# The decay of a Mamba2 mixer: exponents bounded below by zero on GpSimd, one exponential a step on ScalarE

## What is computed

```python
A = -jnp.arange(1, H + 1)                          # 128 heads
dt = jnp.clip(softplus(dt + dt_bias), 0.001, 100)
cs = jnp.cumsum(dA, axis=-1)                       # in chunks of 128 tokens, dA = dt * A
seg = cs[..., :, None] - cs[..., None, :]
Lmat = jnp.where(tri, jnp.exp(seg), 0.0)           # tri: l >= s
scores = jnp.einsum('bclhn,bcshn->bchls', Cc, Bc) * Lmat
Ydiag = jnp.einsum('bchls,bcshp->bclhp', scores, xdt)
# ... the states carried from one chunk to the next, Y = Ydiag + Yoff + x * D
yg = y * silu(gate)
out = (yg * rsqrt(mean(yg ** 2 over a group) + EPS)) * norm_w @ out_proj_w.T
```

## Time and profile before

| | |
|---|---|
| median of three runs | 1798.07 us (1796.7 to 1801.74) |
| span of the profiled execution | 1797.3 us |
| mean granted TensorE clock | 0.981 of full speed |
| instructions | 27181 |
| DMA, mean | 73 GB/s, 131.86 MB |
| length of one group | 206 to 207 us |

### The profile page before, as it was taken

How to read it: one execution, slowest core, us unless ns; L and a number is a source line. 1 busy time by engine, 2 the same in 40 slices (tenths; PEclk the granted TensorE clock), 3 DMA queues, 4 the chain that set the end, 5 groups by cost and what they waited for, 6 DMA issues and landing times. The chain is left out here.

```text
span 1797.3 us, 27181 instructions
## 1 busy us (share of the span) xinstructions
PE 1615.7 (90%) x8296; PEld 1228.1 (68%) x8296; DVE 1479.8 (82%) x1833; ACT 1045.5 (58%) x2144; POOL 1123.3 (62%) x664
## 2 busy tenths in 40 slices
PE   7888989989898899989898898989899898989889
PEld 5666767767676666757676676757676676767666
DVE  6789598986979688895979778895989879895975
ACT  4556574665646565665747665564646666475632
POOL 2039584695828775595928777484936868286831
PEclk9989999999999999999999999999999999999999
DMA  2032221221223122231213222131212312122101
GB/s 107 6 111 93 73 81 56 83 83 54 83 66 100 66 71 77 72 100 53 83 44 105 83 71 77 49 105 60 91 46 83 106 43 90 51 94 82 54 14 70
DMA packets 73672, 131.86 MB, mean 73 GB/s; under 512 B 10944, under 2 KB 10944, under 8 KB 73280
## 3 DMA queue, kind: packets, MB, share of 16 engines
q1 hardware_dynamic: 73536, 130.09, 22.4%
HBM read 127.44 MB, written 2.62 MB: 72 GB/s over the span
## 5 line engine op out<-in xcount | busy, mean ns | idle before, releaser
L161 PE MATMUL bank<-h_hi,mx_w_hi 128*128 128x512 f32 x1152 | 482.2, 419 | 15.5 <-POOL mx_w_lo L834 12.4
L163 PE MATMUL bank<-h_hi,mx_w_lo 128*128 128x512 f32 x1152 | 457.5, 397 | 0.0
L162 PE MATMUL bank<-h_lo,mx_w_hi 128*128 128x512 f32 x1152 | 456.8, 397 | 0.0
L1010 POOL TENSOR_TENSOR mx_y<-mx_y,mx_sg 128x512 f32<-128x512 f32 x128 | 213.4, 1667 | 308.1 <-DVE mx_y L1258 308.1
L887 DVE SCALAR_TENSOR_TENSOR mx_acc<-bank,mx_cw,mx_acc 128x510 f32<-128x510 f32 (+2 forms) x480 | 354.5, 739 | 38.8 <-ACT mx_acc L872 33.9
L1002 POOL TENSOR_TENSOR mx_mix<-mx_csb,mx_mask 128x512 f32<-128x512 f32 x128 | 346.4, 2706 | 3.1 <-DMA mx_csb<-cs_rows 3.1
L1230 DVE TENSOR_TENSOR mx_mix<-mx_mix,mx_cbt 128x1536 f32<-128x1536 f32 x128 | 346.4, 2706 | 0.8
L834 POOL TENSOR_TENSOR mx_w_lo<-mx_w_raw,mx_w_hi 128x512 fp32r<-128x512 f32 x144 | 190.3, 1322 | 209.8 <-ACT mx_w_hi L829 209.8
L161 PEld LDWEIGHTS bank<-h_hi,mx_w_hi 128*128 128x128 f32 x1152 | 220.9, 192 | 77.6 <-issue 35.0
L163 PEld LDWEIGHTS bank<-h_hi,mx_w_lo 128*128 128x128 f32 x1152 | 220.1, 191 | 50.6
L162 PEld LDWEIGHTS bank<-h_lo,mx_w_hi 128*128 128x128 f32 x1152 | 221.1, 192 | 39.7
(11 more groups left out here) (164 smaller groups left out, 2363.8 us busy)
## 6 DMA issues: line engine op xcount, KB each, us to landing
mx_csb<-cs_rows SPq DMA_DIRECT2D x128, 512.0 KB, 3.9
mx_w_raw<-in_w_in SPq DMA_DIRECT2D x144, 256.0 KB, 3.7
mx_wo_raw<-in_w_out SPq DMA_DIRECT2D x64, 256.0 KB, 3.2
res<-in_x SPq DMA_DIRECT2D x8, 256.0 KB, 3.6
f_base_raw<-in_base_wt SPq DMA_DIRECT2D x2, 1024.0 KB, 5.9
out<-res SPq DMA_DIRECT2D x8, 256.0 KB, 2.0
f_a_raw<-in_lora_a SPq DMA_DIRECT2D x2, 256.0 KB, 3.0
f_lb_raw<-in_lora_b SPq DMA_DIRECT2D x2, 256.0 KB, 6.8
```

The source lines that it names most:

```text
L161: nc.tensor.matmul(out, w_hi, x_hi, start=first, stop=False)
L162: nc.tensor.matmul(out, w_hi, x_lo, start=False, stop=False)
L163: return nc.tensor.matmul(out, w_lo, x_hi, start=False, stop=last)
L1010: nc.gpsimd.tensor_tensor(y[:, i, :], y[:, i, :], sg[:, i, :], ALU.mult).then_inc(s["yg"], 1)
```

## The change

GpSimd no longer adds a mask. For each step it writes `max(csb - gncs, 0)` into `mix`, with eight `tensor_scalar` instructions (per head and sequence one of 256 and one of 128 elements; `gncs` is a scalar per partition), and counts `clamped`. ScalarE takes one exponential over the 1536 elements with scale -1 and no bias, in the place of `decay_from_second`; `decay_from_first` goes, and so does `mask_first` on VectorE. Where the target is before the source the exponent is now 0 and the decay 1, and the zero comes from `cbt`: `keep_bc` multiplies by a tensor `causal` of ones and zeros instead of copying. `mix` is stored head first, so that `make_mix` reads one row of 768 for each head. On GpSimd the clamps of the next step stand ahead of `gate_y`. SP's `load_cs` waits for `clamped` instead of `decay`. GpSimd's loop over the groups is written out in full; at a group's end the clamps for the next group wait for its `const`.

```diff
@@ SP
             def load_cs(g, st):
-                step_slot_freed(sp, s["decay"], g, st)
+                step_slot_freed(sp, s["clamped"], g, st)
@@ GpSimd
-            def mask_second(g, st):
-
-                i = st % 2
+            def clamp_exponents(g, st):
+
+                i, j, hf = st % 2, st // 2, st % 2
+                if st == 0:
+                    pool.wait_ge(s["const"], 1 + 5 * g + 3)
                 pool.wait_ge(cs_in[i], 16 * (STEPS // 2 * g + st // 2 + 1))
                 step_slot_freed(pool, s["y"], g, st)
-                rows = csb[:, i, :, :].rearrange("p h (b l) -> p b h l", b=HB)[:, :, :, CH:SEQ]
-                nc.gpsimd.tensor_tensor(mix[:, i, :, :, SEQ:PAIR], rows,
-                                        mask[:, :].unsqueeze(1).unsqueeze(1).to_broadcast([P, HB, 2, CH]),
-                                        ALU.add).then_inc(s["masked1"], 1)
+                for hd in range(2):
+                    for b in range(HB):
+                        tile, head = 2 * (HB * hf + b), 2 * j + hd
+                        nc.gpsimd.tensor_scalar(mix[:, i, hd, b, 0:SEQ], csb[:, i, hd, b * SEQ:(b + 1) * SEQ],
+                                                gncs[:, tile, head:head + 1], 0.0, ALU.subtract, ALU.max)
+                        last = nc.gpsimd.tensor_scalar(mix[:, i, hd, b, SEQ:PAIR],
+                                                       csb[:, i, hd, b * SEQ + CH:(b + 1) * SEQ],
+                                                       gncs[:, tile + 1, head:head + 1], 0.0,
+                                                       ALU.subtract, ALU.max)
+                last.then_inc(s["clamped"], 1)
...
                 for st in range(STEPS + 1):
+                    if st + 1 < STEPS:
+                        clamp_exponents(g, st + 1)
+                    elif st + 1 == STEPS and more:
+                        clamp_exponents(g + 1, 0)
                     if st >= 1:
                         gate_y(g, st - 1)
-                    if st + 1 < STEPS:
-                        mask_second(g, st + 1)
-                    elif st + 1 == STEPS and more:
-                        mask_second(g + 1, 0)
...
-            loop_groups(pool, group)
+            for g in range(NG):
+                group(g, g + 1 < NG)
@@ ScalarE (decay_from_first and decay_from_second are taken out)
+            def decay(g, st):
+
+                i = st % 2
+                act.wait_ge(s["clamped"], 1 + STEPS * g + st + 1)
+                a = mix[:, i, :, :, :].rearrange("p h b l -> p (h b l)")
+                nc.scalar.activation(a, a, ACT.Exp, scale=-1.0).then_inc(s["decay"], 1)
@@ VectorE (mask_first and its calls are taken out)
                 for b in range(HB):
-                    last = nc.vector.tensor_copy(cbt[:, hf, b, :], banks[b][:, 0:PAIR])
+                    last = nc.vector.tensor_tensor(cbt[:, hf, b, :], banks[b][:, 0:PAIR], causal[:, :], ALU.mult)
...
-                a = mix[:, i, :, :, :]
-                nc.vector.tensor_tensor(a, a, cbt[:, hf, :, :].unsqueeze(2).to_broadcast([P, HB, 2, PAIR]),
-                                        ALU.mult).then_inc(s["mix"], 1)
+                a = mix[:, i, :, :, :].rearrange("p h b l -> p h (b l)")
+                both = cbt[:, hf, :, :].rearrange("p b l -> p (b l)").unsqueeze(1).to_broadcast([P, 2, HB * PAIR])
+                nc.vector.tensor_tensor(a, a, both, ALU.mult).then_inc(s["mix"], 1)
```

## The result

| | before | after |
|---|---|---|
| median | 1798.4 us (1796.7 to 1801.7) | 2391.9 us (2391.5 to 2392.5) |
| ratio | | 1.3296, 95% interval 1.3277 to 1.3315 |
| span of the profiled execution | 1797.3 us | 2390.0 us |
| mean granted TensorE clock | 0.981 | 0.874 |

The account below looks back on a forecast made before the run. VectorE, nearly tied with GpSimd, was taken to bound the steps, and GpSimd after the change. 13X - 27.9 us a group at X = 2.8 is +8.5, over 8 groups +68 us: 1865 us, range 1755 to 2000.

Parts of the forecast that it names:

- What bounds the kernel before, and where the bound goes: In the steps, VectorE sets the pace with GpSimd 0.4 to 0.8 us behind; the bound moves to GpSimd.
- what would show it: Signs of being right, such as clamps starting every 0.3 and 0.4 us and steps of 9.9 and 10.4 us.
- X: Total time of the eight tensor_scalar on GpSimd in a step: 2.8 us, likely 1.75 to 4.1.
- The formula: A group changes by 13X - 27.9 us: +8.5 us at X = 2.8, +68 us for 8 groups.
- First half: From skip_y's possible start on step 0 to the first output projection: 7X + 49.3 us against 65.6.
- Second half: From skip_y's possible start on step 9 to the channel sums: 6X + 43.6 against 57.7, plus 2.5 us for the clock.
- The rest of the group stays as is: Outside the two halves, output projections on TensorE with GpSimd idle up to 11.3 us at a time: unchanged.
- y(9): The moment when skip_y can start on the step numbered in the brackets; for step 9 at 433.57 before.
- The memset's pace (1): Rival: the clamps on GpSimd run as fast as a memset, X = 1.56, giving 1717 us; chance 0.15.
- the even case (4): Rival: X on GpSimd lies within 0.05 of 2.15, so the time stays the same; chance 0.05.
- Rival 2: VectorE's hold does not stop one-input GpSimd instructions; TensorE sets the pace, 19.8 us a group saved, 1639 us; chance 0.05.
- Rival 3: The clamps on GpSimd run at the two-input pace, X = 5.3, 2125 us; chance 0.10 for X above 4.1.

Follow-up runs that it names:

- experiment 1: The changed kernel with gate_y put back ahead of the clamps on GpSimd, nothing else: 2311.9 us, ratio to before 1.2842.
- experiment 5: gate_y put first in two kernels: two-input subtractions on GpSimd with Relu on ScalarE (1956.3 to 2006.3 us), and one-operation constant clamps (2149.9 to 2136.3 us).
- experiment 3: The changed kernel with the bound formed by eight Relu on ScalarE, no clamps or mask on GpSimd: 1687.2 us, ratio to before 0.9369.

## Why the prediction was wrong, step by step

*What bounds the kernel before, and where the bound goes*: right. GpSimd without idle time in the steps, VectorE idle before tap 1 for `evacuate`, TensorE waiting more before the transposes (283.5 us against 108.1 in the earlier trace rows) and `make_mix` at 1.75 us, no longer stretched, were all on the list of what would show it.

*X*: the step that failed. It took the affine select as the nearest row because that also reads one tensor and writes one, and allowed 0.05 us each for the scalar and the second operation. The scalar was right within 0.04 us. The second operation costs per element (0.9 ns, thus 0.11 and 0.22 us), and the base was half the true one: 0.25 against 0.49 us at 128. Of the 4.4 us by which X was short, 2.8 are the base (5.20 against 2.44) and 1.6 the scalar and the second operation (2.04, where 0.4 had been allowed). Nor was the two-input pace a ceiling; the text assumed it without a row. 13 x (7.24 - 2.8) x 8 = **462 us of the 527 us** by which the forecast fell short.

*The formula*: a group becomes 206.3 + 13 x 7.24 - 27.9 = 272.5 us; the measured ones are 279.8 (from the channel sums at 363.23 to those at 642.98). For 8 groups the line gives 2328 us. With the measured X it is 2.7% short. Its pieces, in group 2 (the second of eight):

- First half: 7X + 49.3 = 100.0; measured 95.1, from `skip_y` at 406.29 to the projection at 501.39. Second half: 6X + 43.6 + 2.5 = 89.5; measured 87.8. The sums were high, for the larger part because `silu_conv` does not hold a clamp (below), 0.45 us a step. The 0.5 us for that hold was also read high from its own row: 1.66 less 1.27 is 0.39 us.
- "The rest of the group stays as is": failed. From the first projection to y(9) it was 39.3 us and is 53.8. The rows of TensorE's timeline with idle time, at its start and in it:

```profile
501.39 0.79 PE L160 MATMUL bank<-mx_wo_hi,yg_hi 128*128 128x512 f32 x1 [4.93 <-DVE mx_wo_lo L1250]
512.76 0.50 PE L160 MATMUL bank<-mx_wo_hi,yg_hi 128*128 128x512 f32 x1 [2.88 <-ACT gacc L1113]
539.49 0.79 PE L160 MATMUL bank<-mx_wo_hi,yg_hi 128*128 128x512 f32 x1 [6.15 <-ACT gacc L1113]
```

The kernel before waits 2.56 us ahead of its first row of this stretch and not at all inside it. `gacc` is `keep_quad` of ScalarE, which empties the projection's bank; in ScalarE's list it stands behind `round_y`, that waits for `gate_y`, and that stands behind the clamps. These in turn could only start when `mix_tokens` had freed `mix`:

```profile
527.73 1.14 POOL L1005 TENSOR_SCALAR mx_mix<-mx_csb,mx_gncs 128x256 f32<-128x256 f32 x1 [12.98 <-PE bank L1450]
...
536.52 1.25 POOL L1017 TENSOR_TENSOR mx_y<-mx_y,mx_sg 128x512 f32<-128x512 f32 x1
```

```profile
537.81 0.63 ACT L1096 ACTIVATE yg_hi<-mx_y 128x512 fp32r<-128x512 f32 x1 [10.04 <-POOL mx_y L1017]
538.34 0.61 ACT L1104 ACTIVATE mx_sq<-mx_y 128x512 f32<-128x512 f32 x1
538.86 1.06 ACT L1113 ACTIVATE gacc<-bank 128x512 f32<-128x512 f32 x2
```

GpSimd idled 13 us and then did 8.8 us of clamps ahead of the one thing that TensorE needed. That is 9.0 us of waits (2.88 + 6.15), and TensorE's busy time in the stretch is 5.5 us longer (44.74 against 39.27) at a granted clock of 0.85 instead of 0.96: 14.5 together. The prediction named what is queued behind a waiting `gate_y` in an ordinary step and not that `keep_quad` stands in the same list in steps 8 and 9. Experiments 1 and 5 bring these distances down by moving the gate; in experiment 1 the stretch is 40.4 us, with no wait in it.

- Sums to the next y(0): 43.0 us against 44.5.

Group 2 is not typical of the kernel before. It takes 206.8 us there from sums to sums, while four of the seven such distances are 205.2 to 205.4 (the 206 to 207 us of the table ahead of the prediction are the long ones), and its stretch with the projections takes 39.3 us where six of the eight groups take 37.7. Summed over all eight groups, from the same instructions of both traces:

| stretch | after less before, us | the formula with X = 7.24 |
|---|---|---|
| up to the first y(0) | +2.2 | 0 |
| y(0) to the first projection | +236.8 | +275.0 |
| first projection to y(9) | +126.5 | 0 |
| y(9) to the sums | +236.5 | +254.7 |
| sums to the next y(0), or to the end | -9.3 | 0 |
| together | +592.7 | +529.7 |

The stretch that was to stay as it is thus costs 126.5 us, of which the halves, priced too high, hide 56. The 462 us of X and these 63 us make up 525 of the 527.

*The rivals.* The memset's pace (1) and the even case (4) fell with X. Rival 2, one-input instructions that VectorE does not hold, fell: `make_mix` turns 1.12 us into 2.81. Rival 3, the two-input pace and 2125 us, had the right mechanism and was itself 267 us short. It had 0.10 and the range was cut below it; the row that says what a `tensor_scalar` costs was simply not there, and the range of X should have been kept wider above than below. That clamps overlap VectorE's work is half true, below.

*GpSimd's written-out loop and the earlier `load_cs`* were priced at nothing. No run separated either from the clamps. The trace speaks against a cost: the stretches between the groups are 1.2 to 1.7 us shorter than before, and GpSimd's idle time in the groups is all put down to another engine's result. Its one wait for a transfer of `csb` stands ahead of them and is 3.0 us, 3.1 before.

## What to carry to other kernels

An instruction form that the trace does not show has no ceiling in it: two-input work was here the cheaper for an element (1.7 to 1.9 ns against 2.5 and more), and a class of operation that was never timed deserves a range of a factor of two or three, or a run of its own. When work goes ahead of a short instruction in an engine's list, go through the list of every engine that waits for that instruction in each *kind* of step, the rare ones too; what is queued behind it in two of sixteen steps cost 13.4 us a group here, of which moving the gate back gave 10 in all. And ask of a cheap-looking step which engine has both idle time and a cheap form of it: the same eight bounds cost 7.2 us on GpSimd, 4.3 on VectorE beside GpSimd, and 3.0 on a ScalarE that stood at 58%.

## What the runs showed of the hardware

- GpSimd's `tensor_scalar` in f32 costs 2.5 ns an element with one operation and 3.3 to 3.4 with two, plus 0.17 to 0.19 us, and 0.08 us more where its scalar is read from SBUF. `tensor_tensor` with one operand broadcast along the row takes 1.0 us at 512 elements and 1.87 at 1024, which is 1.7 ns an element and 0.13 us.
- A one-input instruction of GpSimd and a two-input instruction of VectorE hold each other unevenly. The clamp at 474.63 takes 2.81 us, as it cannot go on until `make_mix` is through; but `make_mix` starts 0.14 us after it and takes its undisturbed 1.75 us. So do all 120 `make_mix` of this trace that start inside a clamp, even 0.9 us into it: 1.74 to 1.78 us. Beside a two-input GpSimd instruction it takes 2.84 and 2.86 us (experiment 3). `silu_conv` at 474.15 takes 0.70 us beside a clamp of 0.71 that is not stretched either.
- Eight clamps of VectorE take 1.8 us when GpSimd is idle and 4.3 when it isn't: its `tensor_scalar` waits for GpSimd's whole instruction too, although it has only one tensor input.
